# Another order of ScalarE's work around the MLP of a fused state-space and gated-MLP kernel: z of seven quarters one slot later, scales, rounding and first turned copy of h one slot earlier

## What is computed

```python
# block 1: u from the context, z = layernorm(x)
u  = silu(conv1d(ctx @ in_w.T) + conv_b)            # 4 batches, 512 channels, 512 steps
dt, B, C = split(u @ x_proj_w.T); dt = softplus(dt @ dt_w.T + dt_b)
state = state * exp(dt * A) + (dt * u) * B          # 16 states for each channel
y = (sum_n state * C + D * u) * silu(z)
x = x + tanh(g_xattn) * y
# block 2: MLP on layernorm(x)
h = silu(bitlinear(xn, w1)) * bitlinear(xn, w2)     # 512 -> 2048
x = x + tanh(g_ffn) * bitlinear(h, w3)              # 2048 -> 512
```

## Time and profile before

| what | before |
|---|---|
| median of 3 runs | 653.81 us |
| profiled execution | 653.69 us |
| its span, first to last instruction | 651.9 us |
| mean granted clock of TensorE | 0.897 of full |
| GpSimd busy | 587.9 us, 90% |
| VectorE busy | 583.0 us, 89% |
| ScalarE busy | 530.7 us, 81% |
| TensorE matmuls busy | 488.3 us, 75% |

### The profile page before, as it was taken

How to read it: one execution, slowest core, us unless ns; L and a number is a source line. 1 busy time by engine, 2 the same in 40 slices (tenths; PEclk the granted TensorE clock), 3 DMA queues, 4 the chain that set the end, 5 groups by cost and what they waited for, 6 DMA issues and landing times.

```text
span 651.9 us, 7928 instructions
## 1 busy us (share of the span) xinstructions
PE 488.3 (75%) x2560; PEld 296.4 (45%) x2560; DVE 583.0 (89%) x772; ACT 530.7 (81%) x969; POOL 587.9 (90%) x289
## 2 busy tenths in 40 slices
PE   8798878994564678777666486778676887668987
PEld 3254434552553445455534354455454554345543
DVE  6779779997998899999999999989997999999765
ACT  5764767788999778987798797899999898897675
POOL 1399999998999999999999999999999999999431
PEclk9988999997555979999786889889989897978999
DMA  5598587579960100147420100037700000000001
GB/s 186 193 407 309 183 329 276 198 270 389 374 262 0 39 1 2 47 153 276 132 78 0 33 2 17 1 127 244 254 37 1 17 1 18 0 16 18 1 17 48
DMA packets 24472, 80.77 MB, mean 124 GB/s; under 512 B 2464, under 2 KB 5152, under 8 KB 21360
## 3 DMA queue, kind: packets, MB, share of 16 engines
q1 hardware_dynamic: 24432, 80.27, 33.9%
HBM read 72.53 MB, written 7.73 MB: 123 GB/s over the span
## 4 chain that ended last, share of the span: by engine, by line
POOL 30%; DVE 29%; ACT 14%; issue 13%; PE 11%; DMA 2%; SPq 0%; DVEq 0%; POOLq 0%; ACTq 0%
POOL hh L708 15%; POOL hh L818 14%; DVE hh L773 9%; DVE hh L770 8%; DVE room L1048 4%; ACT da L736 3%; DVE sm L1093 2%; PE bank_a L1020 2%; PE bank_b L1029 2%; PE bank_y L851 2%; ACT room L1041 1%; PE da L1211 1%; DVE bank_y L576 1%; DVE sm L904 1%; ACT gbuf L922 1%
## 5 line engine op out<-in xcount | busy, mean ns | idle before, releaser
L773 DVE TENSOR_TENSOR_SCAN hh<-da,hh 128x1024 f32<-128x1024 f32 x85 | 193.4, 2280 | 3.1 <-ACT da L743 3.0
L851 PE MATMUL bank_y<-ident,hh 128*128 128x128 f32 x1024 | 145.3, 292 | 10.8 <-POOL hh L818 8.8
L851 PEld LDWEIGHTS bank_y<-ident,hh 128*128 128x128 f32 x1024 | 129.6, 152 | 40.1 <-issue 17.5
L813 POOL TENSOR_TENSOR hh<-hh,cc 128x1024 f32<-128x1024 f32 x60 | 141.0, 2350 | 0.2 <-ACT hl L756 0.2
L818 POOL TENSOR_TENSOR hh<-hh,cc 128x1024 f32<-128x1024 f32 x57 | 134.2, 2355 | 0.0
L708 POOL TENSOR_TENSOR hh<-pair,bb 128x1024 f32<-128x1024 f32 x30 | 70.5, 2352 | 26.4 <-DMA bb<-xd_scratch 24.2
L770 DVE TENSOR_TENSOR_SCAN hh<-da,hl,hh 128x256 f32<-128x256 f32 x128 | 85.4, 729 | 0.0
L708 POOL TENSOR_TENSOR hh<-wq,bb 128x1024 f32<-128x1024 f32 x32 | 75.3, 2357 | 1.8 <-PE bank_y L851 1.8
L702 POOL TENSOR_TENSOR hh<-wq,bb 128x1024 f32<-128x1024 f32 x32 | 75.1, 2346 | 0.3 <-PE bank_y L851 0.3
L702 POOL TENSOR_TENSOR hh<-pair,bb 128x1024 f32<-128x1024 f32 x32 | 75.2, 2355 | 0.0
L736 ACT ACTIVATE da<-wq,cst 128x256 f32<-128x256 f32 x128 | 53.3, 463 | 12.0 <-DVE hh L770 11.6
(11 more groups left out here) (271 smaller groups left out, 1051.7 us busy)
## 6 DMA issues: line engine op xcount, KB each, us to landing
bb<-xd_scratch SPq DMA_DIRECT2D x32, 512.0 KB, 5.1
cc<-xd_scratch SPq DMA_DIRECT2D x32, 512.0 KB, 6.9
wq<-weights SPq DMA_DIRECT2D x12, 1024.0 KB, 6.5
stage<-weights SPq DMA_DIRECT2D x8, 1024.0 KB, 6.1
xin<-x SPq DMA_DIRECT2D x4, 1024.0 KB, 5.4
room<-weights SPq DMA_DIRECT2D x4, 1024.0 KB, 8.2
u_scratch<-wq SPq DMA_DIRECT2D x6, 512.0 KB, 3.0
wq<-x SPq DMA_DIRECT2D x2, 1024.0 KB, 18.8
```

Of the source, the lines that this page charges most:

```text
L773: ins = v.tensor_tensor_scan(to, da, h, 0.0, ALU.mult, ALU.add)
L813: ins = g_.tensor_tensor(quarters(flat(hh[k % NH])), quarters(flat(hh[k % NH])), cc[:, n:n + 4, t], ALU.mult)
L851: mm = pe.matmul(bank_y[:, (first + c) * P:(first + c + 1) * P], flat(hh[k % NH])[:, at:at + P], ident[:, :], start=False, stop=(s == STEP ...
```

## The change

Nothing is added or taken away: the same instructions stand in another order. (1) z of quarters 5, 7, 8, 9, 10, 13 and 14 is made one slot later, so that its turn comes one slot behind it instead of two; the slots of the turns stay, now written as a table. (2) On ScalarE the copy of turned x stands ahead of z where both are in one slot. (3) GpSimd's power of the mean square moves from slot 7 of a tile to slot 5. (4) VectorE's scales and ScalarE's rounding of h move from slot 7 to slot 6. (5) TensorE's first turn of h and ScalarE's copy of it move from slot 8 to slot 7. Tile 12, whose steps 6 and later stand behind the loop, keeps its place (END - 1). Since one line of the file goes, every line from L487 on is lower by one in the new kernel: L1127 is L1126 there.

```diff
--- before.py
+++ after.py
@@ -479,11 +479,10 @@
             ZA.did(act.activation(zbias_h[:, n], zmr[:, n], ACT.Copy, scale=-0.5), ("scales", b))
 
         def z_slot(i):
-            return (26, 28, 30, 31, 36, 42, 48, 54, 68, 74, 80, 86, 98, 104, 110, 117)[i]
+            return (26, 28, 30, 31, 36, 43, 48, 55, 69, 75, 81, 86, 98, 105, 111, 117)[i]
 
         def z_turn_slot(i):
-            b, q = i // NE, i % NE
-            return z_slot(i) + (1 if b == 0 else 2)
+            return (27, 29, 31, 32, 38, 44, 50, 56, 70, 76, 82, 88, 100, 106, 112, 118)[i]
 
         def z_turned_by(i):
 
@@ -1404,8 +1403,8 @@
                 for k in range(38, 80):
                     if k < ALL and not c_by_vector(k):
                         times_c(g_, k)
-                    for i in range(END):
-                        if k == tile_slot(i) + 7:
+                    for i in range(END - 1):
+                        if k == tile_slot(i) + 5:
                             rh_pool(g_, i)
                     if k + LEAD < ALL:
                         times_b(g_, k + LEAD)
@@ -1517,7 +1516,7 @@
                     if k + LEAD < ALL:
                         exp(act, k + LEAD)
                     for i in range(END - 1):
-                        if k == tile_slot(i) + 8:
+                        if k == tile_slot(i) + 7:
                             hqt_scalar(act, i, 0)
                     for first, n, done in TURNS:
                         if k == done + 3:
@@ -1529,8 +1528,8 @@
                         if k == PAIR[n]:
                             dt_scalar(act, 2 * n)
                             dt_scalar(act, 2 * n + 1)
-                    for i in range(END):
-                        if k == tile_slot(i) + 7:
+                    for i in range(END - 1):
+                        if k == tile_slot(i) + 6:
                             hq_scalar(act, i, 0)
                             hq_scalar(act, i, 1)
                     for i in range(END):
@@ -1542,12 +1541,12 @@
                     for i in TILES:
                         if i >= NE and k == z_turn_slot(i):
                             z_turn_scalar(act, i)
+                    for i in range(END + 1):
+                        if k == tile_slot(i) - 1:
+                            xqt_scalar(act, i)
                     for i in TILES:
                         if k == z_slot(i):
                             z_scalar(act, i)
-                    for i in range(END + 1):
-                        if k == tile_slot(i) - 1:
-                            xqt_scalar(act, i)
                     for first, n, done in TURNS:
                         if k == done + 5:
                             rows_scalar(act, first, min(n, END - first))
```

## The result

The changed kernel takes 676.56 us (median of 4 runs, 674.62 to 676.91) against 654.34 for the kernel before. The ratio is 1.0328, its 95% interval 1.0282 to 1.0374: slower by 3.3% (22.2 us between the medians), where 12.5 us were forecast. The sign was right, the size was not, and 676.6 lies outside the range of 657 to 673.

A forecast was written before the change was run, and what follows sets the result against it. GpSimd's full queue was taken as the bound: its wait at the power's new place, 5.8 us at tile 7, with VectorE's shift reaches 11.4 at tile 11; plus 1.1 push-back, 12.5 on 653.7 gives 666.2 us, range 657 to 673.

The forecast's parts named there:

- The lateness of a single power: GpSimd's power of tile 7 in its new place would wait 5.8 us for ScalarE's mean square.
- the signs named: Waits before L1126 9 to 14 us, at most 6 each; GpSimd busy below 350; L1047 waits 8 or more; tail 44.
- The first passage: Tile 0 to 1: rounding ahead of the next tanh makes VectorE start L1048 at 243.7 us instead of 242.40.
- The term of 9.6 us for eight passages: Rounding ahead of the next tile's tanh delays VectorE 1.2 us at each of eight passages up to tile 9.
- The waits do not add up as long as ScalarE and VectorE keep their own time: At GpSimd's early powers, lateness from one wait shortens the next by as much, with those two engines unmoved.
- the price is the largest, 5.8 us: The early power costs only tile 7's wait, 5.8 us; the later 5.2 and 3.0 are inside it.
- the 1.1 us of feedback in the sum: Late GpSimd products push back on VectorE and TensorE in a few places; 1.1 us added.
- buys nothing there: 0, with 1 us on both sides: z one slot later and the copy of turned x ahead level ScalarE's slots, without effect on the time.
- the second term: Scales and rounding of h one slot earlier delay VectorE; net 6.0 us by tile 9.
- The credit of 3.6 us: VectorE's waits removed by the reorder: 1.1 us for GpSimd's power, 2.5 for tanh behind a rounding.
- The rival that came out at 676.1: VectorE and ScalarE follow GpSimd closely, so each tile pays its own power wait, 22.4 us in all; chance 0.1.
- The rule I set against the forecast: Highest-occupancy engine comes first; the change adds no work to GpSimd, so the time would stay at 653.7 us.

The follow-up runs named there:

- e5: Kernel before with GpSimd's power of tile 7 alone in slot 5 instead of 7; 660.47 us against 655.27, ratio 1.0080.
- e7: Kernel before with seven quarters of z one slot later and nothing else; ratio 1.0052.
- e1: Kernel before with GpSimd's power of tiles 0 to 11 in slot 5 instead of 7; 666.02 us against 653.42, ratio 1.0169.
- e9: Kernel before with GpSimd's power of tiles 7, 9 and 11 in slot 5 instead of 7; 663.96 us against 654.26, ratio 1.0139.
- e4: Kernel before with power, VectorE's scales and ScalarE's rounding of h in slot 6 instead of 7; 669.86 us against 653.42, ratio 1.0240.
- e2: The changed kernel with GpSimd's power in slot 6 instead of 5; 669.48 us, ratio to the kernel before 1.0237.
- e13: Same as e4 but with the power in slot 5 instead of 6; ratio to the kernel before 1.0272.
- e6: Kernel before with only the power and VectorE's scales in slot 6, rounding left in slot 7; 661.28 us against 655.27, ratio 1.0095.
- e12: Kernel before with step 71's product with C on VectorE instead of GpSimd; ratio 1.0022.
- e3: Kernel before with seven z quarters one slot later, copy of turned x ahead of z, last turn in slot 118 instead of 119; ratio 1.0127.
- e11: Kernel before with seven z quarters one slot later and copy of turned x ahead of z, last turn left in slot 119; ratio 1.0132.

## Why the prediction was wrong, point by point

**What held.** GpSimd's full queue as the place where the loss is counted: in every run that lost over 2 us the growth of its waits is within 0.9 us of that of the stretch from step 36's product with C to the last one (22.1 against 22.2 in the change). The lateness of a single power (5.8 worked out, 5.83 measured in e5). The tail (44.1). Of the signs named, GpSimd's busy time below 350, no wait above 6 us and over 8 us before L1047 came; the waits before L1126 are 19.9 us and not 9 to 14. The first passage: L1048 was to start at 243.7 us, 1.2 of it waiting; it starts at 244.73 and waits 1.14:

```profile
244.73 0.69 DVE L1047 SCALAR_TENSOR_TENSOR room<-room,bank_a 128x512 f32<-128x512 f32 x1 [1.14 <-ACT room L1040]
```

This execution was already 1.2 us late ahead of the first moved piece. The agreement is partly luck: z alone makes a wait of the same size there (1.21 in e7), and in the whole change the two don't add up.

The term of 9.6 us for eight passages is near in size: at the first tanh of tiles 1 to 3 and 5 to 9 VectorE waited 10.9 us where it had waited 2.4, so 8.5 more. The whole window's 14.9 - 5.2 = 9.7 is nearer to 9.6, but holds tiles 10 and 12 as well, and less waiting elsewhere.

**First failed step: "The waits do not add up as long as ScalarE and VectorE keep their own time", and so "the price is the largest, 5.8 us".** VectorE doesn't keep it. With the power alone GpSimd waited 11.7 us (e1), and e5 and e9 show the mechanism: behind a delay of GpSimd's of 5.8 us VectorE is 1.6 to 1.8 us late by the second tile after and 3.5 by the fourth, so the next powers are late again. What I took as evidence was that VectorE waited only 1.1 us for GpSimd in the kernel before; that tells how close it was, not how far GpSimd can slip before it waits. For the power alone, the 1.1 us of feedback in the sum should have been 11.7 - 5.8 = 5.9.

**Second: z "buys nothing there: 0, with 1 us on both sides".** z alone is 1.3% slower. I looked at the exponentials, which ScalarE has in reserve, and not at VectorE's z product, whose place in VectorE's queue moved by a slot with ScalarE's and found ScalarE last in its slot, nor at what TensorE does with it: the turn of z stands ahead of the next tile's multiplications and of the sums. How much of the whole change's loss is z's is not settled: nothing between e4 and e2, 0.6% between e13 and the change. The waits for z are in it (6.0 us against 0.9).

**Third: the size of the second term**, scales and rounding: 9.6 - 3.6 = 6.0 us by tile 9 and 8.4 by tile 11. Alone they measure 2.4%, some 16 us (e4). The credit of 3.6 us was not the fault: the wait for the power went (1.1), and the 2.5 us of waits for tanh behind a rounding, 1.7 at tile 9 and 0.7 at tile 10, shrank to 0.5. Tile 9's second tanh before and after the change:

```profile
500.27 0.69 DVE L1048 SCALAR_TENSOR_TENSOR room<-room,bank_a 128x512 f32<-128x512 f32 x1 [1.70 <-ACT room L1041]
```

```profile
516.68 0.69 DVE L1047 SCALAR_TENSOR_TENSOR room<-room,bank_a 128x512 f32<-128x512 f32 x1 [0.50 <-ACT room L1040]
```

What was missing is the way on from a late gated product: it holds up TensorE's multiplications and with them the sums, and GpSimd waits for the buffers. In e4 these waits are 9.8 us; the forecast has no term for them. And VectorE's scales ahead of a scan, which I costed inside the passages, cost 0.95% alone (e6).

**The rival that came out at 676.1.** "The waits add up" has the right time and the right kind of cause: 19.9 us at the power in nine places, where it gave 22.4. That the time agrees is luck. It put six tiles at "no less than 1.2" each; by the same reading of the trace before, these six (2, 4, 5, 6, 8 and 10) are 2.6, 1.5, 3.5, 4.3, 2.8 and 2.3 us late, so all waits taken whole make 32 us and a time near 686. And the waits are not taken whole: the power alone costs some 12 us, and the longest wait in the change is 4.0 us, not 5.8. The rest comes by VectorE's own delay, which keeps the mean squares late for GpSimd: at tile 7 its place is at 466.39 us, 16.2 later than before, and the mean square is done at 469.01 + 0.39 = 469.40, 13.4 later; 5.8 + 13.4 - 16.2 = 3.0, the wait in the timeline above. Both terms of the forecast are in it, and they feed each other.

```profile
469.01 0.39 ACT L1067 ACTIVATE sm<-sm 128x1 f32<-128x1 f32 x1
```

The rule I set against the forecast (the Trainium skill, page "Perfetto Trace Analysis", section "Identifying the Most-Contended Engine": work first on the engine with the highest occupancy) gave, as I read it, no loss, 654; the measurement decides against that reading as a forecast of what reordering costs. e12 bears on it as well: work taken off GpSimd, the busiest engine, did not make the kernel faster.

## What to carry to other kernels

Before moving a piece of a hand-ordered queue, work out for both ends when each engine reaches the new place and when its input is done; that reading was good to 0.1 us. Then don't price a series of waits by the largest, nor by their sum: carry both engines' delays from one place to the next, and give the one that follows a share of the leader's delay (here a third by the second tile and two thirds by the fourth), unless the trace shows a reserve larger than that delay. Where all engines are coupled by short buffers, look also at what stands behind the moved piece's consumers in their queues (here TensorE's sums behind a turn and behind multiplications), since delays grow on that way.

## What was not expected of the hardware

In e4, TensorE's idle time of 3.46 us was followed by matmuls at half speed. The windows of e4 from 271 to 275 and from 275 to 280 us (granted clock is the third figure from the end):

```profile
271.00:275.00 4.00, 0.69 (x7) 0.45 (x5) 2.27 (x3) 4.00 (x7) 4.00 (x2) 0.91 0.00 0
275.00:280.00 5.00, 4.84 (x15) 2.72 (x16) 4.71 (x6) 2.65 (x5) 0.29 (x1) 0.50 0.29 105
```

Before the gap the four matmuls of L1020 took 1.03 us, behind it 1.89, and the eight of L851 took 1.91 instead of 1.04: the clock is at 0.50, the 1.2 GHz level, for three groups, 1.89 + 1.91 + 1.91 less 1.03 + 1.03 + 1.04 is 2.6 us. So up to 2.6 of the 5.25 us at GpSimd come from the clock. The kernel before keeps 1.00 in these same stretches; its longest gap there is 1.67 us. Elsewhere it has the slow level too: behind the 4.76 us of idle time shown above, the four matmuls of L1020 took 1.91 us, in e3 as well as before, so at that passage the clock is no part of e3's loss.

```profile
376.04 1.91 PE L1020 MATMUL bank_a<-wq,xqT 128*128 128x512 fp8e4 x4
```

Over 240 to 600 the mean granted clock fell from 0.91 to 0.86 in the change. The Trainium skill, page "TensorE: Matmul & The Clock Gate", section "🔬 Part 1: The HAM clock gate (the "warmup" mystery)", says that the engine falls to half its clock when it is left idle; the trace agrees. How much of the whole loss the clock makes was not separated. A hint that it may matter is in e11: its four executions took 660.02, 662.20, 663.50 and 664.49 us at mean clocks of 0.898, 0.888, 0.878 and 0.878. The same kernel is slower where the clock is lower; which of the two is the cause these runs don't tell. The profile of e11 is the one of 660.02 us, so its waits are those of the fastest.
